# One routed-expert layer on one core: gate weights spread by TensorE instead of by DMA, and the third routed part moved up

## The reference

```python
def _L0_ffn_ref(x, gate_w, gate_b, w1, w2, w3):      # D_MODEL 64, N_EXPERTS 16, HIDDEN 128
    logits = jnp.einsum('bsd,de->bse', x, gate_w) + gate_b
    probs = jax.nn.softmax(logits, axis=-1)
    top_probs, top_idx = jax.lax.top_k(probs, 2)
    top_probs = top_probs / jnp.sum(top_probs, axis=-1, keepdims=True)
    dispatch = jnp.sum(jax.nn.one_hot(top_idx, n_experts, dtype=x.dtype) * top_probs[..., None], axis=-2)
    h1 = jnp.einsum('bsd,edh->bseh', x, w1)
    h2 = jnp.einsum('bsd,edh->bseh', x, w2)
    hidden = jax.nn.silu(h1) * h2
    expert_out = jnp.einsum('bseh,eho->bseo', hidden, w3)
    return jnp.einsum('bseo,bse->bso', expert_out, dispatch)

h = _L0_tok_ref(x, ...)                               # linear attention with a 1024x1024 mask, PReLU
h = h + _L0_attn_ref(_layernorm(h), ...)              # a scan over the tokens
h = h + _L0_ffn_ref(_layernorm(h), ...)
```

## Time and profile before

| | |
|---|---|
| time, median of 3 runs | 327.31 us (323.82 to 329.04) |
| the profiled execution, span from first to last instruction | 331.5 us |
| PE busy | 257.1 us (78%) |
| PEld busy | 156.7 us (47%) |
| DVE busy | 160.1 us (48%) |
| ACT busy | 119.7 us (36%) |
| POOL busy | 98.2 us (30%) |
| mean granted TensorE clock | 0.846 of full speed |
| DMA packets | 29.74 MB, mean 90 GB/s |

### The profile page before, as it was taken

One profiled execution on the slowest core, in us unless ns is written; L12 is line 12 of the kernel. 1 busy time (PEld: TensorE's weight loads), 2 busy tenths in 40 slices (PEclk: granted clock), 3 DMA queues, 4 the chain that ended last, 5 costly groups with the idle time before them and its releaser, 6 DMA issues.

```text
span 331.5 us, 4678 instructions
## 1 busy us (share of the span) xinstructions
PE 257.1 (78%) x1645; PEld 156.7 (47%) x1645; DVE 160.1 (48%) x283; ACT 119.7 (36%) x283; POOL 98.2 (30%) x119
## 2 busy tenths in 40 slices
PE   8999999988935976258829995169964899952995
PEld 7443332532411323136529884168642698621563
DVE  1453649789805993167705610053410466710664
ACT  1302561764108711467534541022320344311341
POOL 4000000004760077303771047600476000674000
PEclk9999999999985999658965997555796599995699
DMA  7999800000111101332221675995121323021101
GB/s 191 371 388 278 170 0 0 4 0 12 40 51 57 33 20 52 89 95 73 55 58 44 154 160 131 209 222 114 41 59 28 83 65 78 19 44 20 34 16 32
DMA packets 45990, 29.74 MB, mean 90 GB/s; under 512 B 32688, under 2 KB 41072, under 8 KB 45456
## 3 DMA queue, kind: packets, MB, share of 16 engines
q1 hardware_dynamic: 30416, 23.15, 27.1%
q10 hardware_dynamic: 12480, 3.15, 4.3%
q0 software_dynamic: 3072, 3.15, 3.9%
HBM read 20.46 MB, written 8.98 MB: 89 GB/s over the span
## 4 chain that ended last, share of the span: by engine, by line
PE 52%; another core or an unknown queue 19%; ACT 11%; DVE 10%; issue 7%; ACTq 0%; POOL 0%; DVEq 0%; POOLq 0%
PE ring L1013 10%; PE ring L971 9%; PE turn L988 7%; PE side L1025 5%; PE acc L816 4%; PE ring L802 4%; ACT squares L611 3%; PE side L843 3%; DVE mixed L1141 2%; PE ring L759 2%; PE side L775 2%; ACT n L629 2%; PE acc L934 1%; DVE state L1190 1%
## 5 line engine op out<-in xcount | busy, mean ns | idle before, releaser
L559 POOL DMA_INDIRECT slots<-n,slot_i x48 | 47.8, 996 | 121.9 <-DVE slot_i L1256 108.2
L1283 DVE TENSOR_TENSOR act<-ring,silu 128x512 f32<-128x512 f32 x56 | 38.4, 690 | 89.5 <-ACT silu L681 68.6
L569 POOL DMA_INDIRECT back_v<-results,slot_i x48 | 46.5, 968 | 81.4 <-DMA results<-res 67.7
L681 ACT ACTIVATE silu<-ring 128x512 f32<-128x512 f32 x56 | 33.3, 597 | 78.7 <-remote 38.5
L1141 DVE TENSOR_TENSOR mixed<-ring,dg 128x1024 f32<-128x1024 f32 x32 | 38.6, 1218 | 19.5 <-remote 10.9
L816 PE MATMUL acc<-mixed,v 128*64 128x512 f32 x128 | 34.3, 628 | 8.6 <-DVE mixed L1141 8.4
L802 PE MATMUL ring<-kq 64*128 64x512 f32 x128 | 33.5, 629 | 0.0
L1013 PE MATMUL ring<-nT,w_sb 64*128 64x256 f32 x128 | 24.2, 459 | 8.8 <-issue 8.0
L971 PE MATMUL ring<-slots_t,w_shared 64*128 64x128 f32 x192 | 19.8, 328 | 13.7 <-issue 12.7
L988 PE MATMUL turn<-w_sb,act 128*128 128x64 f32 (+1 forms) x192 | 29.1, 314 | 0.0
L988 PEld LDWEIGHTS turn<-w_sb,act 128*128 128x128 f32 x192 | 27.3, 226 | 3.0 <-issue 2.2
(11 more groups left out here) (150 smaller groups left out, 306.5 us busy)
## 6 DMA issues: line engine op xcount, KB each, us to landing
dg<-dgT SPq DMA_DIRECT2D x8, 512.0 KB, 7.8
dg<-given SPq DMA_DIRECT2D x8, 512.0 KB, 15.7
slots<-zeros SPq DMA_DIRECT2D x3, 1024.0 KB, 13.2
w_shared<-w SPq DMA_DIRECT2D x48, 64.0 KB, 2.2
slots<-slots SPq DMA_DIRECT2D x12, 256.0 KB
results<-res ACTq DMA_DIRECT2D x12, 256.0 KB, 2.9
w_sb<-w SPq DMA_DIRECT2D x2, 1024.0 KB, 14.3
xs<-xT SPq DMA_DIRECT2D x4, 256.0 KB, 6.5
```

Source lines behind the costliest of these rows:

```text
L559: pool.indirect_dma_start(out=slots_dram[r], out_offset=bass.IndirectOffsetOnAxis(ap=slot_i[:, r, k, i:i + 1], axis=0), in_=n2[:, u % 2, i ...
L569: pool.indirect_dma_start(out=back_v[:, r, i, k, :], out_offset=None, in_=results_dram[r], in_offset=bass.IndirectOffsetOnAxis(ap=slot_i[: ...
L681: s.activation(silu[:, n % 2], hidden_banks(n)[:, :, 0:PAIRS * P], ACT.Silu).then_inc(silu_done, 1)
L1283: dve.tensor_tensor(act[:, n % ACT_BUFS], hidden_banks(n)[:, :, PAIRS * P:2 * PAIRS * P], silu[:, n % 2], ALU.mult).then_inc(act_done, 1)
```

## The change

`dispatch` is now split by DVE into three bf16 pieces (high, middle and low) that add up to the fp32 value exactly, and put side by side into `pieces`: four more DVE instructions. PE turns them with four bf16 matmuls against an identity (`turn_given`, at pair 6 only), and ACT copies the 128 rows to SBUF once. For each expert one bf16 matmul of 512 columns (`spread_gate`) with a 0/1 matrix `pick` adds the three pieces and spreads them over the 64 partitions of each image, into a PSUM bank. DVE multiplies from there (`weigh`). The DRAM tensor `given` and its ten DMAs are gone. `pick`, the identity in bf16 and the zeros in `pieces` are made by POOL in the space of `xs`, once the projections have read it. The spread and its multiply stand in the first two pieces of pairs 8 to 15. `ITEMS` becomes 24 routed groups and then 32 dense ones, the shared weights of groups 10 and 11 are loaded earlier, and the combines stand earlier.

```diff
-WEIGHTS_AFTER = (-2, -2, -2, -2, -1, 3, 3, 6, 7, 7, 9, 11)
-GIVEN_AFTER = 9
-SPREAD_AFTER = 9
+WEIGHTS_AFTER = (-2, -2, -2, -2, -1, 3, 3, 6, 7, 7, 8, 8)
+GIVEN_PAIR = 6
+FIRST_SPREAD = 8
-GIVEN_PAIRS = (5, 6)
-DENSE_RUNS = (0, 0, 8, 24)
+DENSE_RUNS = (0, 0, 0, 32)
-COMBINE_AFTER = (13, 14, 20, 22, 24, 27)
+COMBINE_AFTER = (11, 13, 15, 17, 21, 24)
...
-                if n == GIVEN_AFTER:
-                    store_given()
-                if n == SPREAD_AFTER:
-                    for i in range(GIVEN_LOADS):
-                        spread_given(i)
...
+            pool.wait_ge(kq_proj, 4 * HALVES)
+            pool.wait_ge(v_proj, 2 * HALVES)
+            pool.memset(pieces[:, :, :, :], 0.0).then_inc(pieces_zeroed, 1)
+            link(pool.tensor_copy(ident_b[:, :], ident[:, :]))
+            link(pool.memset(pick[:, :, :], 1.0))
+            for b in range(BH):
+                half = pick[:, :, rows_b(b)]
+                link(pool.affine_select(out=half, in_=half, compare_op=ALU.is_ge, fill=0.0,
+                                        base=-D * b, pattern=[[-SPLIT, NE], [0, D]], channel_multiplier=1))
+                link(pool.affine_select(out=half, in_=half, compare_op=ALU.is_ge, fill=0.0,
+                                        base=D * b + SPLIT - 1, pattern=[[SPLIT, NE], [0, D]], channel_multiplier=-1))
...
-            def turn_given(b):
+            def turn_given():
                 pe.wait_ge(dispatch_done, 1)
-                if b == 0:
-                    pe.wait_ge(h_done, UNITS)
-                else:
-                    pe.wait_ge(nT2_done, 1)
+                pe.wait_ge(h_done, UNITS)
+                pe.wait_ge(pick_done, 1)
                 for t in range(TT):
-                    mm = pe.transpose(given_bank(b)[:, t * P:(t + 1) * P], dispatch[:, 0, t * BH + b, :], ident[:, :])
+                    mm = pe.matmul(given_bank[:, t * P:(t + 1) * P], pieces[:, t].rearrange("p b c -> p (b c)"), ident_b[:, :],
+                                   start=True, stop=True)
                 mm.then_inc(given_turned, 1)
+
+            def spread_gate(e):
+                pe.wait_ge(given_done, 1)
+                pe.wait_ge(nT2_done, 1)
+                if e >= 2:
+                    pe.wait_ge(weighed_done, e - 1)
+                if e == NE // 2:
+                    pe.wait_ge(sin_done, ROUTED // 2)
+                pe.matmul(spread_bank(e), pick[:, e, :], given_t[:, :], start=True, stop=True).then_inc(spread_out, 1)
...
+                if piece in (0, 1) and 0 <= 2 * (i - FIRST_SPREAD) < NE:
+                    spread_gate(2 * (i - FIRST_SPREAD) + piece)
...
-                dve.tensor_tensor(dispatch[:, 0], dispatch[:, 0], dispatch[:, 1], ALU.add).then_inc(dispatch_done, 1)
+                link(dve.tensor_tensor(dispatch[:, 0], dispatch[:, 0], dispatch[:, 1], ALU.add))
+                dve.wait_ge(pieces_zeroed, 1)
+                rest, left = (dispatch[:, k].rearrange("p (t b) e -> p t b e", b=BH) for k in range(2))
+                high, mid, low = (pieces[:, :, :, n:SPLIT * NE:SPLIT] for n in range(SPLIT))
+                link(dve.tensor_copy(high, rest))
+                link(dve.tensor_tensor(left, rest, high, ALU.subtract))
+                link(dve.tensor_copy(mid, left))
+                dve.tensor_tensor(low, left, mid, ALU.subtract).then_inc(dispatch_done, 1)
...
             def weigh(e):
-                dve.wait_ge(ld_given[e // (NE // GIVEN_LOADS)], 16 * BH)
+                dve.wait_ge(spread_out, e + 1)
+                dve.wait_ge(mixed_done, ALL_STEPS)
                 dve.wait_ge(nT2_done, 1)
-                dve.tensor_tensor(weighed[:, e, :], weighed[:, e, :], nT2[:, :], ALU.mult).then_inc(weighed_done, 1)
+                dve.tensor_tensor(weighed[:, e, :], spread_bank(e), nT2[:, :], ALU.mult).then_inc(weighed_done, 1)
...
-                if piece in (0, 1):
-                    if 2 * i + 2 in DENSE_POS[:NE]:
-                        weigh(DENSE_POS.index(2 * i + 2) + piece)
+                if piece in (0, 1) and 0 <= 2 * (i - FIRST_SPREAD) < NE:
+                    weigh(2 * (i - FIRST_SPREAD) + piece)
```

More of the change, by code:

```diff
@@ L107 @@
 RES_BUFS = 2
-GIVEN_LOADS = 4
+SPLIT = 3
 LEAD = 2
-DENSE_RUNS = (0, 0, 8, 24)
+DENSE_RUNS = (0, 0, 0, 32)
 FIRST_TURN = 18
@@ L291, in build_layer @@
         dispatch = sb("dispatch", [P, 2, UT, NE])
-        given_t = mixed[0:NE, 0]
+        pick = xs[:, 0, :].bitcast(BF16).rearrange("p (e m) -> p e m", e=NE)
+        spare_xs = xs[:, 1, :].bitcast(BF16)
+        pieces = spare_xs[:, 0:CW].rearrange("p (t b c) -> p t b c", b=BH, c=D)
+        given_t = spare_xs[:, CW:2 * CW]
+        ident_b = spare_xs[:, 2 * CW:2 * CW + P]
         sum_t = sb("sum_t", [P, 2, CW // 2])
@@ L345, in build_layer @@
         x_turned, nT2_done = sem("x_turned"), sem("nT2_done")
+        pieces_zeroed, pick_done = sem("pieces_zeroed"), sem("pick_done")
         dispatch_done, given_turned, given_done = sem("dispatch_done"), sem("given_turned"), sem("given_done")
-        given_stored, ld_given, weighed_done = sem("given_stored"), [sem(f"ld_given{i}") for i in range(GIVEN_LOADS)], sem("weighed_done")
+        spread_out, weighed_done = sem("spread_out"), sem("weighed_done")
         sum_done, sum_turned, summed = sem("sum_done"), sem("sum_turned"), sem("summed")
@@ L372, in build_layer, with spread_bank @@
         x_bank = side[:, 0, :]
-        def given_bank(b):
-            return side[0:NE, 1 - b, :]
+        given_bank = side[:, 1, :]
+        def spread_bank(e):
+            if e % 2 == 1:
+                return side[:, 1, :]
+            return side[:, 0, :] if e < NE // 2 else acc[:, :]
         def turned_sum(c):
@@ L699, in expert_piece @@
                     take_x(DENSE_UNIT)
-                if piece == 1 and i in GIVEN_PAIRS:
-                    take_given(GIVEN_PAIRS.index(i))
+                if piece == 1 and i == GIVEN_PAIR:
+                    take_given()
                 if piece == 3:
@@ L1046, in expert_piece @@
                     turn_x(DENSE_UNIT)
-                if piece == 0 and i in GIVEN_PAIRS:
-                    turn_given(GIVEN_PAIRS.index(i))
+                if piece == 0 and i == GIVEN_PAIR:
+                    turn_given()
+                if piece in (0, 1) and 0 <= 2 * (i - FIRST_SPREAD) < NE:
+                    spread_gate(2 * (i - FIRST_SPREAD) + piece)
                 if piece == 2 and 1 <= i <= ALL_PAIRS:
```

21 lines of the change are left out of this document (5 added, 16 removed).

## The result

| | before | after |
|---|---|---|
| median | 327.21 us (323.82 to 329.04, 4 runs) | 339.32 us (336.70 to 340.63, 4 runs) |
| profiled execution, span | 331.5 us | 338.5 us |
| PE / DVE / ACT / POOL busy | 257.1 / 160.1 / 119.7 / 98.2 us | 264.5 / 161.2 / 119.0 / 104.5 us |
| mean granted TensorE clock | 0.846 | 0.843 |
| DMA packets | 29.74 MB | 25.48 MB |

The ratio is 1.0389 [1.0303, 1.0475]: 12 us slower, where 3.5 us faster was forecast, and above the range of 316.5 to 334.

A forecast was written before the change was run, and what follows sets the result against it. From 185 us on mostly PE was taken to bound the kernel, with three stalls at the gathers. From the median 327.31, -0.8 - 4.2 - 5.9 + 4.4 + 3.0 = -3.5 gave 323.8 us, range 316.5 to 334.

The forecast's parts named there:

- Turning the gate weights: On PE, four bf16 matmuls replace two groups of four fp32 transposes: -0.8 us, on the path.
- The first stall: PE's stall in gather 0, 18.7 us, shortens without the broadcast by 2.1 to 6.2 us; -4.2 taken.
- The clock behind it: TensorE's half clock after the first stall falls from 17.9 to 6.2 us: -5.9 us, ends 0 and -5.9.
- Sixteen spreads: Sixteen added bf16 matmuls on PE, 0.244 us each by the warm-up's price: +4.4 us, bounds 3.5 to 8.1.
- The chain on DVE: Multiplies waiting for spreads delay gated products in dense pairs 12 to 15: +3.0 us, ends 0 and 4.9.
- enough: In a routed pair, PE's 1.93 us of results behind its hidden products were said to cover DVE's multiplies.
- What I let the second stall hide: Pair 12 and most of 13, at half clock behind that stall, hide DVE's chain: 4.6 us becomes +3.0.
- Order: Routed groups moved ahead, 32 dense ones after, gathers 1 and 2 starting earlier: 0 us.
- their stalls stay: Gathers 1 and 2, moved earlier, keep their stalls of 11 to 12 us and the clock behind them: 0.
- the load is innocent: Rival: broadcast touches neither first stall nor clock, gains 0, costs stay: +6.6, 333.9 us; chance 0.20.
- a rule that said so: Trainium skill, SBUF section: engine and DMA ports are disjoint, neither slows the other; the prediction went against it.

The follow-up runs named there:

- b1: Kernel before without the ten DMAs of the gate weights and the waits on them (not the true gate weights): 325.20 us, ratio 0.9992 [0.9947, 1.0037].
- b0: The kernel before, unchanged, run and profiled a second time: 328.80 us, ratio 1.0102 [0.9969, 1.0235], span 327.8.
- f1: Kernel before in the changed kernel's order, without broadcast DMAs and without spreads, on a chip with stops: 332.52 us, ratio 1.0061 [1.0004, 1.0117].
- the mended one: Changed kernel with DVE's multiplies behind the gated products and combines moved out of pairs 12 to 15: 254.17 and 253.88 us on the chips without stops.
- d3: Kernel before with each part's 16 gathers in four bunches that wait for PE's progress: 260.73 us, ratio 1.0044, on a chip without stops.
- a2: Changed kernel with only spreads 0 and 1 of 16, DVE's instructions and order kept: 332.86 us, ratio 1.0156 [1.0112, 1.0199].
- e4: Kernel before with gathers in bunches of four that wait for given pairs, on another chip without stops: 260.67 us, ratio 1.0015 [0.9968, 1.0062].

## Why the prediction was wrong

Two terms failed, the gain at the first stall and the gain in the clock behind it: -10.1 us of the sum, measured as nothing. The costs, +6.6 by the sum, came to some 12. In the order of its steps, for the kind of chip of the result:

- **Turning the gate weights, -0.8.** Right: four bf16 transposes stand in 0.33 us on PE in place of two groups of 0.54, -0.75. POOL's new work shows nowhere: gather 0 starts at 195.31 after and at 194.43 before, at 196.61 in the repeated kernel before.
- **The first stall, -4.2. This failed.** b1's interval leaves -1.7 to +1.2 us for this term and the next one together. The stall is 17.6 us long without a broadcast, and with one 18.7 in the first execution of the kernel before and 15.8 in b0. (Three executions with the broadcast have PE idle for 12.0 to 13.7 us in the 27 us from gather 0's start, six without it for 9.8 to 13.0: a us or so may be in it, but not in the time.) The prediction took the longest of three stalls of a single execution and gave its length to what stood beside it. The row that spoke against it (PE slows before the first big DMA is issued) was in the prediction and was right.
- **The clock behind it, -5.9. This failed too, and was the largest term.** Measured 0, within the same interval. The half clock ended at 237 in one execution of the kernel before and by 227 in the next. One profile doesn't tell how long the clock takes to come back.
- **Sixteen spreads, +4.4.** The size was off: 0.32 each at the full clock and not 0.244, 5.1 us in all. The warm-up's small matmuls were the wrong row; the bounds of 3.5 to 8.1 held it.
- **The chain on DVE, +3.0.** The working was right for the dense pairs (0.46 and 1.98 measured, 0.4 and 1.9 worked out). It missed that the combine at routed pair 11 makes PE wait too, 1.26: "enough" in its sentence on the routed pairs was wrong there. In all 5.7 undisturbed, 4.6 worked out. What I let the second stall hide was not worth it: the half clock behind it hides pair 12's wait in the result's trace, but the third stall then takes more.
- **Order, 0.** Off by 2 us (f1). And "their stalls stay" failed for the third: it had lain over pairs without spreads, and with gather 2 moved up it begins right behind pairs 14 and 15, where it costs PE 2 to 3 us more.

The range was also drawn too narrow by its own terms: with each uncertain term at its dear end the sum is -0.8 - 2.1 - 0 + 8.1 + 4.9 = +10.1, or 337.4 us, not the 329 that the prediction gives for it.

With the gains at zero the account is f1's +2.0 (order, broadcast out), and 10.7 from there to the changed kernel (1.0389 less 1.0061 of 327 us), of which about 5 are spreads, 2 to 3 the longer third stall, and the rest, 3, the chain: +12.7 for the measured +12.1. Only the sums are measured by repeated runs; the split rests on single executions.

So the rival "the load is innocent" was the right one, with the condition as stated (gains under 6.6) and a price of 12 and not 6.6. It had 0.20; a rule that said so and a row that said so deserved more than one that was read from an accident.

On the two chips without stops the sign of each half is another: the gain is real (9 to 10 us) and the cost is much the same (9 to 11), so the changed kernel is level with before (1.0106 [0.9992, 1.0220]), and the mended one is faster on both, 0.9702 and 0.9822. No complete kernel that was tried beats the kernel before on the chips with stops.

Open stays why the gathers stop the engines on some chips and not on others, and whether the paced gathers of d3 would help where they do; both runs with them fell on the other kind. Of the 1.6% left in a2, f1 has 0.6%; the remaining 1%, about what the third stall takes more, wasn't measured apart from DVE's order and the place of the multiplies.

## What to carry to other kernels

An oddity of a single profile (the longest of three stalls, the longest spell at half the clock) is no term of a sum until a second execution shows it. Ask of a wait that is to be removed what else covers the same time: here a stall lay over it, so the removal was worth 9 to 10 us on one kind of chip and nothing on the other, while the instructions added for it cost some 10 on both. Work that hangs on PE (here the multiply of a spread) belongs on DVE behind the product for which PE waits: that order, together with the combines moved out of those pairs, was worth 5 to 8 us where nothing else lay over it.

## What the runs showed of the hardware

- The same kernel takes 260 us on two chips and 327 to 330 on the others. The difference is in the runs of indirect DMAs on POOL, which go at 1.25 us each on both. On one kind PE, DVE and ACT go on beside them. On the other, in nine executions, PE begins to stop some 4 to 10 us into a run of gathers and is back 1 to 5 us behind its end; in between single matmuls come 0.3 to 2.5 us apart (first gather), and a hand-over from one engine to another can take 5 to 7 (third gather). Without the 48 gathers the kernel before drops to 0.86 on the second kind.
- The scatters do it too. Up to 60 us both kinds give PE the same 57.57 us of work; in the first run of 16 scatters it gets 15.13 of 24.20 us on a chip that stops (the kernel before) and 22.07 on one that doesn't (e4, which is the same kernel up to there):

```profile
78.10:102.30 24.20, 15.13 (x74) 6.16 (x74) 12.59 (x14) 3.84 (x20) 15.56 (x16) 0.89 0.12 38
```

```profile
78.00:102.20 24.20, 22.07 (x106) 8.59 (x106) 20.89 (x35) 11.06 (x52) 15.55 (x16) 1.00 0.22 66
```

- Nothing in the rows looks like a slow port: the late instructions take their usual time (0.69), and PE and ACT are held as well. The same section of the Trainium skill, "SBUF: two separate sides", names only DVE and GpSimd as engines that hold each other up; no run here shows that in these stalls.
- A bf16 matmul of 512 columns in a row of fp32 ones took 0.32 us of PE's time at the full clock and 0.54 at half of it.
- The time at half the clock behind the same stall of the same kernel was 8 us in one execution and 18 in another.
